# The query side of an attention block: row maxima turned by DMA, output product slot by slot

## The reference, cut to what matters

```
q   = x_normalised.T @ Wq.T              # positions x (8 heads x 64), from LayerNorm(x)
qh  = softmax(q, axis=features of a head) / 8
ctx = softmax(keys).T @ values           # made before, on the key side
out = Wo @ (ctx^T qh) + bo
out = out / max(norm(out over the 64 rows), 1e-12) * g * 8
x   = x + out
```

## Time and profile before

| | |
|---|---|
| median of three runs | 874.47 us (871.25 to 878.85) |
| the profiled execution | 871.09 us |
| its span, first to last instruction | 869.3 us |
| mean granted TensorE clock | 0.923 of full |
| busy: TensorE, VectorE, ACT, GpSimd | 742.1, 644.8, 509.9, 278.1 us |
| the query side | about 522 to 765 us of the span |

### The profile page before, as it was taken

How to read it: one execution, slowest core, us unless ns; L and a number is a source line. 1 busy time by engine, 2 the same in 40 slices (tenths; PEclk the granted TensorE clock), 3 DMA queues, 4 the chain that set the end, 5 groups by cost and what they waited for, 6 DMA issues and landing times. The chain is left out here.

```text
span 869.3 us, 16469 instructions
## 1 busy us (share of the span) xinstructions
PE 742.1 (85%) x5987; PEld 407.4 (47%) x6013; DVE 644.8 (74%) x1052; ACT 509.9 (59%) x928; POOL 278.1 (32%) x230
## 2 busy tenths in 40 slices
PE   0988984769999769999999996999999999849944
PEld 0776763734444324545554552444444444325532
DVE  7264667969999657777777746999999999555447
ACT  1254993647777446766676643878778787622201
POOL 1452425101112100000000004676777767434200
PEclk9997995789999969999999996999999999969965
DMA  7596210013434200000000000000000000024305
GB/s 224 140 289 185 51 28 1 1 43 73 70 78 71 55 13 25 26 15 24 25 26 13 14 1 0 2 1 1 1 1 1 2 1 2 0 49 80 67 1 193
DMA packets 82371, 41.13 MB, mean 47 GB/s; under 512 B 73428, under 2 KB 73428, under 8 KB 82292
## 3 DMA queue, kind: packets, MB, share of 16 engines
q1 hardware_dynamic: 79184, 31.49, 15.7%
q0 software_dynamic: 2144, 8.46, 2.7%
q10 hardware_dynamic: 964, 0.13, 0.1%
HBM read 23.81 MB, written 4.19 MB: 32 GB/s over the span
## 5 line engine op out<-in xcount | busy, mean ns | idle before, releaser
L1298 POOL TENSOR_TENSOR query_qn<-query_eq,query_rq 128x1024 f32<-128x1024 f32 x64 | 121.7, 1902 | 56.9 <-DVE query_rq L1232 54.9
L1076 ACT ACTIVATE keys_ek<-keys_psK,keys_mk 128x512 f32<-128x512 f32 x128 | 86.8, 683 | 50.1 <-DVE keys_mk L1027 46.6
L1027 DVE TENSOR_REDUCE keys_mk<-keys_psK 128x2 f32<-128x1024 f32 x64 | 78.4, 1225 | 39.0 <-PE keys_psK L1115 38.2
L1223 DVE TENSOR_REDUCE query_mq<-query_psQ 128x16 bf16<-128x1024 f32 x64 | 75.6, 1181 | 5.6 <-PE query_psQ L1366 5.4
L1229 DVE TENSOR_REDUCE query_lq<-query_eq 128x16 f32<-128x1024 f32 x64 | 77.2, 1207 | 2.2 <-ACT query_eq L1307 2.1
L1307 ACT ACTIVATE query_eq<-query_psQ 128x1024 f32<-128x1024 f32 x64 | 65.2, 1019 | 22.5 <-PE query_psQ L1379 22.5
L1126 PE MATMUL keys_psT<-all_ident,keys_ek 128*128 128x128 f32 x512 | 71.2, 283 | 0.0
L1388 PE MATMUL query_psX<-all_ident,query_qn 128*128 128x128 f32 x512 | 70.8, 282 | 0.0
L1126 PEld LDWEIGHTS keys_psT<-all_ident,keys_ek 128*128 128x128 f32 x512 | 55.9, 143 | 28.6 <-issue 26.8
L1138 PE MATMUL keys_psG<-keys_eT,keys_cT 128*64 128x512 f32 x256 | 69.0, 618 | 0.0
L1314 ACT ACTIVATE query_qT<-query_psX 128x1024 f32<-128x1024 f32 x64 | 65.5, 1023 | 1.2 <-PE query_psX L1388 1.2
(11 more groups left out here) (269 smaller groups left out, 1549.3 us busy)
## 6 DMA issues: line engine op xcount, KB each, us to landing
all_x_res<-in_x_dram SPq DMA_DIRECT2D x4, 1024.0 KB, 9.5
all_ctx_n<-in_ctx_dram SPq DMA_DIRECT2D x32, 128.0 KB, 3.7
all_cf<-in_ctx_dram SPq DMA_DIRECT2D x16, 256.0 KB, 2.7
out_dram<-all_x_res SPq DMA_DIRECT2D x16, 256.0 KB, 2.2
all_raw_d<-in_L_ffn_w_down_dram POOLq DMA_DIRECT2D x4, 688.0 KB, 8.9
all_raw_g<-in_L_ffn_w_gate_dram POOLq DMA_DIRECT2D x5, 512.0 KB, 5.1
all_raw_u<-in_L_ffn_w_up_dram POOLq DMA_DIRECT2D x5, 512.0 KB, 7.5
all_w_nat<-in_L_ffn_W_dram SPq DMA_DIRECT2D x4, 256.0 KB
```

Source lines behind the costliest of these rows:

```text
L1027: dve.tensor_reduce(mk[:, c, :], psK[c % 2][:, :, :], X, ALU.max, negate=True).then_inc(mk_ok, 1)
L1076: act.activation(ek[t % 2][b][:, c, :], psK[c % 2][:, b, :], ACT.Exp, bias=mk[:, c, b:b + 1], accum_out=le[t % 2][:, b, c:c + 1]).then_inc ...
L1223: dve.tensor_reduce(mq[g % 2][:, :, 0:HEADS], psQ[g % 2][:, :, :].rearrange("p b (h d) -> p b h d", d=D), X, ALU.max, negate=True).then_in ...
L1298: pool.tensor_tensor(qn[m % 2][:, :, :], eq[m % 3][:, :, :], rq[m % 2][:, :].unsqueeze(2).broadcast_to([P, 2 * HEADS, D]), ALU.mult).then_ ...
```

## The change

The loop's order and what some steps read and write are changed:

- The maxima are turned by a DMA transpose that SP issues per slot, from a 128x128 bf16 tile (of which 64 columns carry something) straight into mT. TensorE's transpose into psR and ACT's copy are gone, and so is the PSUM bank psR.
- The output product is made per slot, with 128 columns, into the slot's quarter of one of two banks psF. qT holds one slot, in three buffers; qn has three buffers too.
- The inverse norm is written back into psF by ACT, and z reads it from there.
- The low part of x is made by GpSimd.
- The steps stand at other distances: sums and qn two slots behind (was one), transposes four (was three), output product six, then y, squares, inverse norm and z of a tile at slots 10, 11, 11 and 12 counted from the tile's first, residual at 13, statistics at 17. TensorE's order in a slot is queries(g), product(g-6), fold(g-1), squares, transposes(g-4).

```diff
-        mq = [s.sb(f"mq{p}", [P, 2, 32], BF16) for p in range(2)]
-        mT = [s.sb(f"mT{p}", [D, P], BF16) for p in range(2)]
+        mq = [s.sb(f"mq{p}", [P, 4, 32], BF16) for p in range(2)]
+        mT = [s.sb(f"mT{p}", [P, 1, P], BF16) for p in range(2)]
...
-        psR = s.ps("psR", [D, P], BF16)
-        psF = s.ps("psF", [P, 512])
+        psF = [s.ps(f"psF{p}", [P, 512]) for p in range(2)]
...
+        SUM, TURN, OUT = 2, 4, 6
+        LAST = SLOTS + 14
+        def tile_at(g, after):
+            u, c = (g - after) // NC, (g - after) % NC
+            return u if c == 0 and 0 <= u < TILES else None
+        @block.sync
+        def _(sp):
+            for g in range(SLOTS):
+                sp.wait_ge(mq_ok, g + 1)
+                wait(sp, f_ps, g - 1)
+                sp.dma_start_transpose(mT[g % 2][:, :, :], mq[g % 2][:, :, :].rearrange("p b n -> p (b n)")).then_inc(
+                    mT_in[g % 2], 16)
         @block.vector
...
             def queries_max(g):
                 dve.wait_ge(q_ps, g + 1)
-                wait(dve, r_ps, g - 1)
+                wait(dve, mT_in[g % 2], 16 * (g // 2))
...
-                dve.scalar_tensor_tensor(out=z[:, :], in0=inv[:, :], scalar=1e12, in1=y[:, :], op0=ALU.min,
+                dve.scalar_tensor_tensor(out=z[:, :], in0=psF[u % 2][:, :], scalar=1e12, in1=y[:, :], op0=ALU.min,
...
             for g in range(LAST):
                 if is_slot(g):
                     queries_max(g)
+                if (u := tile_at(g, 12)) is not None:
+                    normalised(u)
+                if is_slot(g - SUM):
+                    sums(g - SUM)
+                if (u := tile_at(g, 17)) is not None:
+                    stats(u)
         @block.gpsimd
...
+            def low(t):
+                pool.wait_ge(hi_ok, t + 1)
+                wait(pool, q_ps, NC * (t - 1))
+                pool.tensor_tensor(xs_lo[t % 2][:, :], xn[:, :], xs_hi[t % 2][:, :], ALU.subtract).then_inc(lo_ok, 1)
...
             for g in range(LAST):
                 t, c = g // NC, g % NC
+                if t + 1 < TILES:
+                    if c == 0:
+                        normed(t + 1)
+                    if c == 1:
+                        high(t + 1)
+                    if c == 2:
+                        low(t + 1)
+                if is_slot(g - SUM):
+                    normalised(g - SUM)
+                if (u := tile_at(g, 13)) is not None:
+                    result(u)
         @block.scalar
...
-            def shift(g):
-                act.wait_ge(r_ps, g + 1)
-                wait(act, f_ps, g - 1)
-                act.activation(mT[g % 2][:, :], psR[:, :], ACT.Copy).then_inc(mT_ok, 1)
...
+                act.activation(psF[u % 2][:, :], ln[:, :], ACT.Exp, scale=-0.5, bias=k.half_ln[:, :]).then_inc(inv_ok, 1)
...
                 if is_slot(g - 1):
                     exponentials(g - 1)
+                if is_slot(g - TURN):
+                    transposed(g - TURN)
+                if (u := tile_at(g, 10)) is not None:
+                    result(u)
+                if (u := tile_at(g, 11)) is not None:
+                    inverse(u)
         @block.tensor
...
-            def shift(g):
-                pe.wait_ge(mq_ok, g + 1)
-                wait(pe, mT_ok, g)
-                pe.transpose(psR[:, :], mq[g % 2][:, :, :].rearrange("p b n -> p (b n)"), k.ident16[:, :]).then_inc(r_ps, 1)
             def fold(g):
-                pe.wait_ge(mT_ok, g + 1)
+                pe.wait_ge(mT_in[g % 2], 16 * (g // 2) + 16)
...
+            def out(g):
+                t, c = g // NC, g % NC
+                pe.wait_ge(qT_ok, g + 1)
+                wait(pe, z_ok, t - 1)
+                for j in range(NC):
+                    for b in range(2):
+                        mm = pe.matmul(chunk(psF[t % 2], c)[HALF[b], :], k.M[:, 2 * t + b, j, :], qT[g % 3][:, b * NC + j, :],
+                                       start=j == 0, stop=j == NC - 1, skip_group_check=True)
+                mm.then_inc(o_ps, 1)
...
             for g in range(LAST):
                 if is_slot(g):
                     queries(g)
+                if is_slot(g - OUT):
+                    out(g - OUT)
                 if is_slot(g - 1):
                     fold(g - 1)
+                if (u := tile_at(g, 11)) is not None:
+                    squares(u)
+                if is_slot(g - TURN):
+                    turn(g - TURN)
```

More of the change, by code:

```diff
@@ L1185, in query_side @@
         rq = [s.sb(f"rq{p}", [P, 2 * HEADS]) for p in range(2)]
-        qn = [s.sb(f"qn{p}", [P, 2 * HEADS, D]) for p in range(2)]
-        qT = [s.sb(f"qT{p}", [P, 2 * NC, L]) for p in range(2)]
+        qn = [s.sb(f"qn{i}", [P, 2 * HEADS, D]) for i in range(3)]
+        qT = [s.sb(f"qT{i}", [P, 2 * NC, P]) for i in range(3)]
         y = s.sb("y", [P, L])
@@ L1279, in high, with result, normalised @@
                 pool.tensor_scalar(xs_hi[t % 2][:, :], xn[:, :], 1.0, 0.0, ALU.mult, ALU.add).then_inc(hi_ok, 1)
+            def low(t):
+                pool.wait_ge(hi_ok, t + 1)
+                wait(pool, q_ps, NC * (t - 1))
+                pool.tensor_tensor(xs_lo[t % 2][:, :], xn[:, :], xs_hi[t % 2][:, :], ALU.subtract).then_inc(lo_ok, 1)
+            def result(u):
+                pool.wait_ge(z_ok, u + 1)
+                pool.tensor_tensor(k.x[:, u, :], k.x[:, u, :], z[:, :], ALU.add).then_inc(x_ok, 1)
+            def normalised(m):
+                pool.wait_ge(rq_ok, m + 1)
+                wait(pool, x_ps, m - 2)
+                pool.tensor_tensor(qn[m % 3][:, :, :], eq[m % 3][:, :, :],
+                                   rq[m % 2][:, :].unsqueeze(2).broadcast_to([P, 2 * HEADS, D]), ALU.mult).then_inc(qn_ok, 1)
             pool.wait_ge(k.rs.rstd_ok, 3)
@@ L1283, in _ @@
             high(0)
+            low(0)
             for g in range(LAST):
                 t, c = g // NC, g % NC
[L1286 to L1299, removed]
-                                       ALU.mult).then_inc(qn_ok, 1)
+                if t + 1 < TILES:
[9 more added lines that the diff above has]
+                    result(u)
         @block.scalar
@@ L1368, in queries @@
                 mm.then_inc(q_ps, 1)
[L1370 to L1373 removed]
             def fold(g):
[L1376 removed]
+                pe.wait_ge(mT_in[g % 2], 16 * (g // 2) + 16)
                 for b in range(2):
                     rows = slice(32 * b, 32 * b + 32)
[L1379 removed]
+                    mm = pe.matmul(psQ[g % 2][:, b, :], mT[g % 2][rows, 0, :], k.ind[rows, :], start=False, stop=True,
                                    skip_group_check=True)
@@ L1388, in turn @@
                         mm = pe.transpose(psX[:, b, j * P:(j + 1) * P],
-                                          qn[g % 2][:, b * HEADS + 2 * j:b * HEADS + 2 * j + 2, :].rearrange("p h d -> p (h d)"),
+                                          qn[g % 3][:, b * HEADS + 2 * j:b * HEADS + 2 * j + 2, :].rearrange("p h d -> p (h d)"),
                                           k.ident[:, :])
                 mm.then_inc(x_ps, 1)
-            def out(t, j):
-                if j == 0:
-                    pe.wait_ge(qT_ok, NC * t + NC)
-                    wait(pe, ln_ok, t)
-                for b in range(2):
-                    mm = pe.matmul(psF[HALF[b], :], k.M[:, 2 * t + b, j, :], qT[t % 2][:, b * NC + j, :], start=j == 0,
-                                   stop=j == NC - 1)
-                if j == NC - 1:
-                    mm.then_inc(o_ps, 1)
+            def out(g):
[7 more added lines that the diff above has]
+                mm.then_inc(o_ps, 1)
@@ L1403, in _, with squares @@
+            def squares(u):
+                pe.wait_ge(y_ok, u + 1)
+                pe.wait_ge(sq_ok, u + 1)
+                pe.matmul(psF[u % 2][:, :], k.blk[:, :], sq[:, :], start=True, stop=True).then_inc(ss_ps, 1)
             for g in range(LAST):
-                t, c = g // NC, g % NC
                 if is_slot(g):
                     queries(g)
+                if is_slot(g - OUT):
+                    out(g - OUT)
                 if is_slot(g - 1):
                     fold(g - 1)
-                if is_slot(g - 3):
-                    turn(g - 3)
```

69 lines of the change are left out of this document (11 added, 58 removed).

## The result

The changed kernel takes 886.64 us (median of 4 runs, 882.97 to 888.98) where the kernel before takes 874.86 (4 runs, 871.25 to 878.85): 1.013 times as long, 95% interval 1.007 to 1.019. The profiled execution took 882.97, its span is 881.1 us, its mean granted clock 0.923 as before. So the change costs about 12 us; 875 was forecast, in a range of 865 to 890.

The account below looks back on a forecast made before the run. VectorE was taken as the bound, TensorE just behind. Start +3.4, steady +0.7 and end -2.0 gave +2.1 on the profiled 871.09, 873.2; the forecast was put at 875 us, range 865 to 890.

Parts of the forecast that it names:

- a late transfer: Rival, slower: folds wait for the DMA transpose of the maxima; 886 to 888 us at 3.10 us latency; chance 0.18.
- start +3.4: First slots of the query side: no product covers the transfer's latency, so queries(7) start later; +3.4 us taken.
- steady +0.7: Steady stretch: four plain slots take 12.88 for 13.85 us, then 13 tiles at +0.13 each; +0.7 us.
- end −2.0: After the last queries: shorter last product, -2.5, its exponential behind the inverse norm, +0.5; together -2.0 us.
- What takes VectorE's place is PE and ACT in lockstep: Steady slots: TensorE and ScalarE wait on each other; plain slot 3.22 us, tile 13.98 against 13.85.
- the ring: Steady slots: fold, exponential, freed PSUM bank, queries, product, next fold; 1.50 + 0.75 + 0.97 = 3.22 us a plain slot.
- So VectorE sets the pace: Steady stretch before the change: VectorE bounds it, 189.4 us busy of 193.9, with TensorE just behind.
- the fast rival: Steady slots: TensorE packs fully, never held by exponentials or squares; tile 13.2 us, total 860 to 865; chance 0.19.
- The product in quarters: Output product per slot, 16 passes of 128 columns, 0.97 us a slot; costs 0.34 us more a tile.
- T: Time from the end of the maximum to the fold's start via DMA transpose; 2.3 us taken, range 2.0 to 3.1.
- z, low part, norm: z reading PSUM takes 0.62 us, low part on GpSimd 1.28, inverse norm written to PSUM 0.71.
- The last output product is a quarter: −2.5: End of the query side: last output product takes 0.97 us for 3.5, saving 2.5 us.

Follow-up runs that it names:

- e10: Changed kernel with the inverse norm written to SBUF again and read from there by z; 884.13 us, one run.
- e12: Kernel before, with the low part of x on GpSimd and a tile's statistics moved behind the first slot's sums on VectorE; 874.20 us, ratio 1.000.
- e1: Changed kernel with the exponentials taken over only half of the columns, 512 of 1024; 888.96 us, one run.
- e5: Changed kernel with y, square, Ln and Exp placed ahead of the copy of the transposed queries on ScalarE; 879.49 us, ratio 1.011.
- e7: Changed kernel with the fourth output product of each slot moved behind the transposes, transfers kept; 890.64 us, one run.
- e3: Kernel before with only the low part of x moved from VectorE to GpSimd; 870.83 us, ratio 0.999.
- e11: Changed kernel with the fourth product behind the transposes and, on ScalarE, the copy of transposed queries last; 875.85 us, ratio 1.006.
- e8: Changed kernel with the output product 512 columns wide for a whole tile, one feature chunk a slot, later steps two slots later; 892.62 us, one run.
- e4: Kernel before with only the maxima turned by DMA transpose, TensorE's transpose and ACT's copy of them gone, order untouched; 896.33 us, ratio 1.026.

## Why the prediction was right or wrong

**The mechanism was right for the steady slots, the size too small, and the end went the other way.** The sum said +2.1 on the profiled execution, which gave +11.9. "Within 1%" had the largest chance, 0.53, and the time came out 1.3% slower, for which there was 0.29, mostly for a late transfer, which did not happen in the steady slots. It lies within 865 to 890 only because that rival had widened the range. As far as the number goes, this is luck. By stretch: start +3.4 forecast in one term, +0.4 ahead of Q0 and +3.2 in Q0 to Q7 found (the +0.6 of the first low part has no place of its own in the sum); steady +0.7 forecast, +6.2 found; end −2.0 forecast, +3.3 found; the other stages took 1.3 off.

Not all of the 3.2 is the order's. The granted clock in Q0 to Q7 was 0.61, for 0.67 before, and there is the fold that waited 0.58. e10 took 23.7 at 0.71 and e12, whose order is the one before, 21.7 at 0.69: 2.0 apart.

**"What takes VectorE's place is PE and ACT in lockstep" held**; the ring is the one described, and e1, e5 and e7 each shorten it at a different place. Its terms were mis-sized. The handover from the exponential to the queries was an estimate, 0.05, and is 0.14. The product to the next fold was read off the key side as 0.97 and is 1.03. With 0.01 for the exponential, a plain slot is 3.38 for 3.22. The slot of squares came out at 4.17 for 4.21, the one after at 3.43 for 3.33. Counted as the prediction did, 13 tiles at 0.38 and four plain slots at 0.16, that is 5.6 us, for 5.5 missed.

**"So VectorE sets the pace" was wrong** (e3). Two engines stood at 189 and 190 us of 193.9, and I took the one that had the waits of others. The time for which z and the low part were held looked like work; the text itself had seen that GpSimd held them. The mistake did not enter the sum, which was built on TensorE's and ScalarE's starts, but it fed the fast rival ("VectorE gets 2 us free a tile"), which had 0.19. That rival fails besides by its own terms: with TensorE full a tile takes 13.99 (e11), not 13.2, because the split product costs 1.18 in place of 0.97.

**The product in quarters:** forecast 3.88 a tile for 3.54, it is 4.12. e8 shows that the width has no part in it. The Trainium skill ("TensorE: Matmul & The Clock Gate", section "Back-to-back issue gap") would have had 1.30 a slot; the measured 1.03 decides against it, as the key-side row had.

**The transfer** came at T = 2.32 to 2.37 where TensorE waited for one that nothing disturbed (2.3 taken). In the steady stretch only three folds have a wait for it at all, 0.5 us together, all of the weight load and none of the matmuls. Its rival, at 0.18, was not what happened, though 886 to 888 is where the time fell: the right time for another reason. e1 shows how near it is: with a ring 0.26 shorter, the slow transfers take back more than the ring gave.

**z, low part, norm:** z took 0.69 and the low part 1.16 (1.28 taken), the norm 0.69 (0.71). That z would be short was right, that PSUM would be the reason is not borne out (e10). As neither is on the path, none of it shows in the time, but for the first low part: 0.44 of the 0.6 forecast.

**"The last output product is a quarter: −2.5" was the worst step.** The product is shorter, but the last tile's y does not wait for it. The end of the changed kernel (timeline of ScalarE and VectorE):

```profile
767.26 0.59 ACT L1338 ACTIVATE query_ln<-query_psF 128x512 f32<-128x512 f32 x1
...
767.89 0.69 ACT L1340 ACTIVATE query_psF<-query_ln,all_half_ln 128x512 f32<-128x512 f32 x1
...
768.61 0.69 DVE L1242 SCALAR_TENSOR_TENSOR query_z<-query_psF,query_y 128x512 f32<-128x512 f32 x1 [7.67 <-ACT query_psF L1340]
...
769.40 0.78 ACT L1331 ACTIVATE query_y<-query_psF,query_gbo,all_g 128x512 f32<-128x512 f32 x1 [0.82 <-DVE query_z L1242]
```

There is one y buffer, so y of tile 15 waits for z of tile 14, and that stands behind the norm of tile 14, its squares, and copies of the slots after. The pipeline is deeper, and y of the last tile begins 19.48 us after Q63 (749.92 to 769.40), where before it was 16.25. From there to the end both take the same, 7.0 and 6.9. With y and square ahead of the copy (e5) 2.6 us of this go. I had counted how much less work the last product is, not what the engine does between it and the end. Some 0.75 more is a fold that waited for a slow transfer, at 755.93.

**What stays open.** The sum for the end had no term for the deeper pipeline; e5 takes back 2.6 us of it, and the rest was not taken apart by a run. What TensorE loses when it turns to the product and away (0.885 a chunk in one visit, 1.01 alone; 1.03 in one piece, 1.18 in two) was not measured by itself. And no run shows what does bound the kernel before.

## What to carry to other kernels

A busy share counts the time in which an instruction is held; before giving an engine relief, take one of its steps away, or look for whom it keeps waiting. When a bound is removed, write out the ring that takes its place, with every handover, since the 0.09 and 0.06 us missed here come in nearly all of 56 slots. A deeper pipeline is paid for at both ends of its stage, so follow the last tile instruction by instruction there.

## What the runs showed of the hardware

The transfer has two lengths. From the end of the maximum to the start of a fold that waits for it, it is mostly 2.3 us. The Trainium skill ("DMA: Bandwidth & Descriptors", section "Anatomy of one DMA — SWDGE (gpsimd) path") puts the fixed part of a transfer at about 2.0 on GpSimd's path; no run here uses that path, and this transfer, issued by SP, mostly lands in 2.2. But some land only after up to 4.4. In the changed kernel, e1, e4, e5 and e7 to e11 there are 576 transfers. In 435 of them no packet of an instruction queue (q8 or q14) was under way in the first 2.2 us from the issue; they landed in 2.20 to 2.35 us. In the other 141 there was one, and 60 of those took more than 2.5 us, the longest 4.42. No transfer was slow without such a packet; most of the slow ones, 54, had one of q8, which are of 16 KB. The slowest one of the changed kernel, first the fold, then the DMA queues from 752.03 to 755.93 (packets, MB, share of 16 engines):

```profile
755.93 0.39 PE L1371 MATMUL query_psQ<-all_ind,query_mT 32*128 32x512 bf16 x2 [0.75 <-DMA query_mT<-query_mq]
```

```profile
q1 hardware_dynamic: 160, 0.03, 4.9%
q8 instruction: 1, 0.02, 2.3%
...
query_mT<-query_mq SPq DMA_TRANSPOSE x1, 3.8
```

That these packets are loads of program code, and that they delay the small transfer, is a reading of the queue's name and of times that coincide; no run moved or removed one.
